# Four full-array matmuls of 512 columns ahead of each quad of value products in a two-stage attention on one Trainium2 core

## The reference

```
nx = _ada_rmsnorm(x, time_emb, w_norm1, ...)
q = (nx @ wq + bq).reshape(b, s, 16, 8)      # k and v alike
q = q * cos + _rotate_half(q) * sin           # k alike
scores = jnp.einsum('bshd,bthd->bhst', q, k) / jnp.sqrt(8.0)
probs = jax.nn.softmax(scores, axis=-1)
attn = jnp.einsum('bhst,bthd->bshd', probs, v).reshape(b, s, 128)
x = x + attn @ wo + bo
```

## Time and profile before

| | |
|---|---|
| median of 3 runs | 551.28 us (545.5 to 555.97) |
| the profiled execution | 551.2 us |
| its span, first to last instruction | 549.4 us |
| mean granted TensorE clock | 0.785 of full speed |
| PE busy / DVE busy / ACT busy / POOL busy | 399.7 / 371.7 / 265.3 / 126.0 us |

### The profile page before, as it was taken

One profiled execution on the slowest core, in us unless ns is written; L12 is line 12 of the kernel. 1 busy time (PEld: TensorE's weight loads), 2 busy tenths in 40 slices (PEclk: granted clock), 3 DMA queues, 4 the chain that ended last, 5 costly groups with the idle time before them and its releaser, 6 DMA issues.

```text
span 549.4 us, 7499 instructions
## 1 busy us (share of the span) xinstructions
PE 399.7 (73%) x2472; PEld 258.7 (47%) x2473; DVE 371.7 (68%) x937; ACT 265.3 (48%) x753; POOL 126.0 (23%) x124
## 2 busy tenths in 40 slices
PE   5899999999988797576868677888993441054564
PEld 5656575676565566234435344544452331013353
DVE  4389688879899473648766957411159649979794
ACT  1564656865745343334473455433432762275252
POOL 1000000000000072402927723000663003372101
PEclk9999999999999979675576778565698555555597
DMA  8930000000000000000000000000000000000001
GB/s 324 431 150 2 1 0 2 2 0 1 2 0 1 1 2 0 0 0 1 1 1 2 2 1 1 1 0 1 1 0 0 1 0 1 0 0 1 1 0 39
DMA packets 3837, 13.41 MB, mean 24 GB/s; under 512 B 372, under 2 KB 2420, under 8 KB 3284
## 3 DMA queue, kind: packets, MB, share of 16 engines
q1 hardware_dynamic: 3800, 12.93, 5.9%
HBM read 12.41 MB, written 0.52 MB: 24 GB/s over the span
## 4 chain that ended last, share of the span: by engine, by line
PE 52%; DVE 27%; ACT 11%; issue 7%; POOL 1%; DMA 1%; POOLq 0%; SPq 0%; ACTq 0%; DVEq 0%
PE bank L913 6%; ACT big L525 5%; PE bank L933 4%; PE bank L961 4%; PE bank L947 4%; PE bank L1139 3%; DVE area L1405 3%; DVE nmax L1706 3%; PE bank L975 3%; PE bank L1084 3%; PE bank L918 3%; DVE area L1408 3%; DVE tab_ L1405 2%; ACT area L525 2%; PE bank L1032 2%
## 5 line engine op out<-in xcount | busy, mean ns | idle before, releaser
L525 ACT ACTIVATE big<-bank,nmax 128x256 f32<-128x256 f32 x128 | 59.2, 473 | 29.8 <-DVE nmax L1557 16.3
L525 ACT ACTIVATE area<-bank 128x512 f32<-128x512 f32 (+4 forms) x84 | 43.4, 520 | 59.2 <-PE bank L918 16.2
L525 ACT ACTIVATE big<-bank 128x512 f32<-128x512 f32 (+1 forms) x84 | 41.0, 516 | 52.3 <-PE bank L1112 28.2
L1706 DVE TENSOR_REDUCE nmax<-bank 128x2 f32<-128x512 f32 x64 | 41.2, 685 | 29.1 <-PE bank L1084 28.9
L1565 DVE COPY area<-bank 128x512 f32<-128x512 f32 x64 | 42.4, 684 | 10.2 <-PE bank L947 10.2
L442 POOL TENSOR_TENSOR rstd<-rstd,halves 128x2 f32<-128x2 f32 x4 | 2.8, 698 | 182.5 <-DVE rstd L1408 182.5
L947 PE MATMUL bank<-tabs,big 128*128 128x128 f32 x256 | 37.6, 278 | 7.9 <-DVE big L1408 7.9
L1557 DVE TENSOR_REDUCE nmax<-bank 128x2 f32<-128x512 f32 x64 | 41.6, 683 | 0.4 <-PE bank L933 0.4
L947 PEld LDWEIGHTS bank<-tabs,big 128*128 128x128 f32 x256 | 29.8, 141 | 23.6 <-DVE big L1408 14.2
L1408 DVE TENSOR_SCALAR big<-big,rrec 128x256 f32<-128x256 f32 x128 | 36.5, 349 | 1.1
L913 PE MATMUL bank<-xT,w0s 128*128 128x256 f32 x128 | 33.9, 396 | 4.2 <-issue 4.2
(11 more groups left out here) (226 smaller groups left out, 909.0 us busy)
## 6 DMA issues: line engine op xcount, KB each, us to landing
w2s<-w SPq DMA_DIRECT2D x1, 4352.0 KB, 26.6
rows<-row SPq DMA_DIRECT2D x1, 1600.0 KB, 11.2
w0s<-w SPq DMA_DIRECT2D x3, 512.0 KB, 7.1
w1s<-w SPq DMA_DIRECT2D x1, 1408.0 KB, 16.2
w0s<-w SPq DMA_DIRECT2D x1, 1024.0 KB, 13.3
tabs<-tab SPq DMA_DIRECT2D x1, 549.5 KB, 5.5
xs<-x SPq DMA_DIRECT2D x1, 512.0 KB, 4.2
out<-tab_ SPq DMA_DIRECT2D x2, 256.0 KB, 2.3
```

Source lines behind the costliest of these rows:

```text
L525: return nc.scalar.activation(o, i, f, **kw)
L1706: V.tensor_reduce(nmax[:, n // 8, :, n % 8], bank[n % 2][:, :].rearrange("p (q k) -> p q k", q=QT), AX, ALU.max, negate=True).then_inc(S(" ...
```

## The change

In `values1(g)` the wait for bank 4 to be free (`a1_o`, from group 1 on) comes first. Then stand four new matmuls: stationary `kaT[:, g % 4, 0:128]`, moving `kaT[:, g % 4, 0:512]`, all 128 rows and all 128 columns of the array, 512 columns moved, float32r, into the whole of bank 4. Then comes the wait for the exponentials (`a1_exp`), and then the value products, which start bank 4 anew. Nobody reads what the four matmuls write. There are 16 groups, so 64 new matmuls.

```diff
             def values1(g):
 
-                pe.wait_ge(S("a1_exp"), 4 * g + 4)
                 if g >= 1:
                     pe.wait_ge(S("a1_o"), g)
+                for u in range(4):
+                    mm(bank[4][:, :], kaT[:, g % 4, 0:P], kaT[:, g % 4, 0:512], start=True, stop=True)
+                pe.wait_ge(S("a1_exp"), 4 * g + 4)
                 for k in range(QT):
                     for n in range(4 * g, 4 * g + 4):
```

## The result

The changed kernel takes 557.44 us (median of 4 runs, 555.56 to 559.9). The kernel before, timed beside it, took 548.39 us (4 runs, 542.56 to 555.97). The ratio is 1.021 with a 95% interval of 1.011 to 1.031. Every ratio with an interval in this document is taken over those runs of each kernel that lie within about 1.5% of its fastest, while the medians are over all runs. The change makes the kernel slower. On which side of 2% the change lies stays open. The profiled execution took 558.1 us, its span 556.3 us.

What follows compares the result with a forecast made beforehand. PE was taken to bound most of the kernel, often at the low clock. Passes of 24.0 us, less 5.3 hidden and 13.3 given back by the clock, add 5.4 us to 551.2: 556.6 us, range 540 to 573 us.

Steps and rivals of the forecast that it cites:

- What bounds the kernel: Whole kernel: PE holds 52% of the chain of waits; in the quads VectorE often waits for PE, 19.4 us for scores.
- Cost of the passes: Quads: groups of four passes take 1.68 us (12 low) or 0.96 us (4 high), 24.0 us of PE time.
- rival 3: Quads: a full-array float32r pass costs like a float32 one, 88 us for 64, 640 us in all; chance 0.02.
- Hidden part: Behind groups 1, 2, 3, 5 and 10 PE's idle time hides 5.3 us of the passes, leaving 18.7 us exposed.
- The waits: The moved waits for exponentials and bank 4 cost 0; at most they give back 1.5 us at group 15.
- Give-back: Quads: the clock rises at five groups (1.8 us each) and value products run high at five (0.86 each), 13.3 us.
- Sum: Whole kernel: 18.7 - 13.3 = +5.4 us on 551.2 us, giving 556.6 us, +1.0%.
- its cases: Whole kernel's outcome, with 2% as about what can be told from no change: faster 0.12, same 0.55, slower 0.33.
- The tail: Behind 376 us, after the quads: taken as 0, with 3 us saved or lost as bound.

Runs made afterwards that it cites:

- e1_strip: The changed kernel with the same 64 new matmuls, each using only 32 of the array's 128 rows; 577.49 us, ratio 1.047.
- e4_waits: The changed kernel with both waits (exponentials and bank 4) ahead of the new matmuls; 558.93 us, ratio 1.024.
- e7_tail: The kernel before with eight full-array passes of 512 columns at one place, ahead of the last transposes of outputs; 542.74 us, ratio 0.993.
- e10_tail_four: The kernel before with four full-array passes of 512 columns at one place, ahead of the last transposes of outputs; 543.51 us, ratio 0.991.
- e5_idle: The kernel before with 46 full-array passes of 256 columns, put only where PE idles for VectorE; 547.57 us, ratio 1.000.
- e9_tail_idle: The kernel before with 46 passes of 256 columns ahead of waits for VectorE and eight of 512 at the attention's tail; 546.98 us, ratio 0.986.

## Why the prediction was right

**What bounds the kernel.** Right. PE is on the chain in the quads, L1136 with 16.7% of it, and VectorE idles for PE: 19.4 us before, 23.4 after. I had said this idle time would change little; it grew by 4.0 us, more than half of the stage's 6.5.

**Cost of the passes.** 24.0 us predicted, 24.1 measured, but that is luck: two errors cancel. Four passes take 2.01 and 1.12 us, not 1.68 and 0.96: the step between passes in the burst, where two heads run side by side, was too short a model. The number of rows is not the reason, since strips of 32 rows took the same in e1_strip; what the difference is was not tested. With the prediction's 12 low and 4 high groups these prices give 12 x 2.01 + 4 x 1.12 = 28.6 us. Fewer groups ran low than that in the changed kernel, so the 24.1 us already hold some 4.5 us of what the clock gave back. That a float32r pass over the full array does not cost as a float32 one (rival 3) is plain from the same rows.

**Hidden part.** 5.3 us predicted, and over the whole stage PE's idle time fell by 0.3 us only. At groups 5 and 10 it went as said: the idle time behind them shrank from 1.92 to 1.02 us and from 1.82 to 0.69 us, with 1.3 and 1.1 us of passes, and the distance from group to group grew by 0.14 and 0.01 us. The distance at group 1 changed by -0.07 us, but not for the reason given: its idle times are 0.80 and 1.58 us, as before, and the passes took the place of time that its value products gave up by running high (1.01 us instead of 1.92). At group 3, where 1.0 us was to be hidden, the distance grew by 0.96 us, and the 1.02 us wait for VectorE is still there (299.09). At other places PE's waits grew, among them those for the parts of a batch (1.70 to 2.17 us) and for the maxima two bursts behind group 10 (1.49 to 1.96 us), and this took back what groups 5 and 10 had hidden.

**The waits.** Priced at 0, shown by e4_waits. At group 15 the new matmuls came behind the wait for bank 4, 1.45 us at 382.25, as said.

**Give-back.** 13.3 us predicted. Measured by PE's busy time in the two traces, 24.1 us were added and 6.7 us came out, so 17.4 us were given back by the clock; against the shorter stages that the old code took in e7_tail and e10_tail_four, with PE busy for 79.4 and 80.4 us, it is 12 to 13 us. The prediction had counted only value products and bursts. In the two traces the value products gave back 6.8 us (28.6 to 21.8; 8.6 predicted) and all that the prediction had left out (the projections, the transposes and the small chain) 6.4 us, so that some 4 us are left for the bursts, which it had put at 4.7. The clock of 0.81 against "near 0.8" agrees, and e1_strip shows the mechanism the other way: the same passes on 32 rows cost 24 us of stage, 18 us more than full-array ones, with the clock no higher than before. The rule of the Trainium skill that busyness releases the clock ("TensorE: Matmul & The Clock Gate", section "What's actually happening") is too plain for this kernel: with strips PE was busier (117 of 134 us) at a lower clock (0.59).

**Sum.** 24.1 - 17.4 = +6.7 us of busy time with idle time unchanged, +6.5 us of stage, against +5.4 predicted; against the mean of the four stages with the old code, 108.3 us, it is +8.0 us. The term of hidden time was too large by 5.0 us and that of given-back time too small by up to 4.1; in this pair of traces they cancel. The time, 557.44 us against 556.6, is nearer than the sum deserves for another reason too: the forecast starts from 551.2 us, and the kernel before, timed beside the changed one, took 548.39. The measured change by the medians is +9.1 us, or 1.7%, and not 1.0%. What was right is the direction, the mechanism (a cost of about 24 us of which the clock gives back half or more), and the range. Two slips in the recorded text changed nothing in this: slice 15 of the clock reads 0.7, not 0.9, and the shares that it gives its cases add up to 0.10 for faster and 0.36 for slower, not 0.12 and 0.33.

**The tail.** Taken as 0 with 3 us either way; in the two traces it gave 2.1 us back, and its first stretch took 17.87 us instead of 20.90. That is within what traces of the same code differ by, so the term is not refuted. But the row of 18.5 us of PE work at 0.50 was the one place where such passes paid, as e7_tail shows, and the prediction did not see that in it.

## What to carry to other kernels

In this kernel unread full-array passes paid where a long stretch of PE's own work ran low behind them (2.3 us of passes, the stretch 6.6 us shorter in the trace, the kernel 0.7% faster over 12 runs). They did not pay between short bursts that wait for other engines, where each pass cost about 0.1 us net at two, four and eight per group. One kernel shows this, and other kernels have to be measured. Test the mechanism with the same passes on fewer rows: the cost stays, the effect goes. In a kernel whose clock moves between its levels, stage lengths in single traces differed by 3.5 us with the same code. So compare many runs, read the clock beside them, and profile the old code more than once before a term of a few us is called measured.

## What the runs showed of the hardware

PE made busier with 32-row passes ran at a lower clock than without them: 0.59 with PE busy for 87% of the stage (e1_strip), 0.67 with 77% (before). With the same number of passes on 128 rows it ran at 0.81, busy for 78%. A float32r pass of 512 columns took 0.50 us at 1.2 GHz and 0.28 us at 2.4 GHz in a group of four, and about the same with 32 rows. At the tail, four such passes (375.67 to 377.03 us in e10_tail_four, partly at each level) gave the kernel the same time as eight. The level, once high, held through four-row products (4*128, 2.20 us for six records against 4.20 at 1.2 GHz) to 388 us and beyond with PE never idle in that stretch of e7_tail; it fell in four-row products or right behind them in one execution each of e5_idle, e9_tail_idle and e10_tail_four. What decides between these stays open.
